# Gathered rows and finished messages in separate buffers in the edge loops of a four-layer graph network, on one core

## The reference, cut to what matters

```python
# layer 0 (the edge's message is a function of both ends and of one edge feature)
x_ = jnp.concatenate([h[src], h[dst], e], axis=1)
m = jax.nn.relu(x_ @ W1 + b1) @ W2 + b2
h_new = jax.ops.segment_sum(m, dst, num_segments=n)

# layer 1
msg = jax.nn.relu(x[src] + edge_attr @ We + be)
aggr = jax.ops.segment_sum(msg, dst, num_segments=n)
h = (1.0 + eps_gin) * x + aggr          # then a small MLP and norms

# layers 2 and 3: x = A x, three and ten times, with A the weighted adjacency
msgs = norm[:, None] * x[row]
x = jax.ops.segment_sum(msgs, col, num_segments=n)
```

## Time and profile before

| | us |
|---|---|
| median of 3 runs | 3231.95 (3231.12 to 3231.97) |
| the profiled execution, its own time | 3232.12 |
| its span in the profile | 3230.3 |
| edge loop of layer 0, 101 superblocks | from about 50 to 1137 |
| edge loop of layer 1, 101 superblocks | from about 1175 to 2194 |
| layers 2 and 3, dense | from about 2260 on |

### The profile page before, as it was taken

How to read it: one execution, slowest core, us unless ns; L and a number is a source line. 1 busy time by engine, 2 the same in 40 slices (tenths; PEclk the granted TensorE clock), 3 DMA queues, 4 the chain that set the end, 5 groups by cost and what they waited for, 6 DMA issues and landing times.

```text
span 3230.3 us, 59857 instructions
## 1 busy us (share of the span) xinstructions
PE 2794.5 (87%) x18663; PEld 1855.0 (57%) x18663; DVE 1793.9 (56%) x3704; ACT 415.6 (13%) x1074; POOL 1158.0 (36%) x1229
## 2 busy tenths in 40 slices
PE   6888888898888858888888888885899999999998
PEld 5677667777777746666666666664333333333333
DVE  4666666666666647777767777774865211111113
ACT  2111111111111111111111111111001000000000
POOL 4355555555555525555555555550000000000000
PEclk9899999989998979999999999996899999999999
DMA  4122222222212232222222222220899999999998
GB/s 115 24 47 48 46 48 48 46 49 46 48 35 46 49 52 60 60 60 60 60 60 60 60 61 61 61 59 5 298 365 337 340 348 343 351 352 353 350 351 279
DMA packets 376595, 447.32 MB, mean 138 GB/s; under 512 B 154575, under 2 KB 193589, under 8 KB 373290
## 3 DMA queue, kind: packets, MB, share of 16 engines
q1 hardware_dynamic: 323834, 376.76, 36.0%
q0 software_dynamic: 38784, 39.79, 6.4%
q10 hardware_dynamic: 13920, 30.00, 2.5%
HBM read 416.03 MB, written 30.36 MB: 138 GB/s over the span
## 4 chain that ended last, share of the span: by engine, by line
PE 44%; issue 18%; SPq 17%; DVE 9%; another core or an unknown queue 8%; DVEq 2%; DMA 1%; ACT 1%; ACTq 0%
PE bank L1652 25%; PE bank L1472 8%; SPq L518 5%; SPq L521 4%; SPq L509 3%; PE bank L1495 3%; SPq L505 2%; PE bank L1625 2%; PE bank L1484 1%; PE bank L1463 1%; DVE arena L860 1%; PE bank L1656 1%; DVE arena L810 1%; SPq L499 1%
## 5 line engine op out<-in xcount | busy, mean ns | idle before, releaser
L1472 PE MATMUL bank<-arena 128*128 128x320 bf16 x6090 | 891.7, 303 | 54.2 <-DVE arena L810 40.4
L1652 PE MATMUL bank<-arena 128*64 128x512 f32 (+1 forms) x4368 | 891.5, 543 | 35.8 <-DVE arena L1062 33.3
L1472 PEld LDWEIGHTS bank<-arena 128*128 128x128 bf16 x6090 | 596.9, 99 | 317.5 <-DVE arena L810 53.6
L646 POOL DMA_INDIRECT arena<-d_p,arena x606 | 572.8, 945 | 539.3 <-issue 384.4
L646 POOL DMA_INDIRECT arena<-d_t,arena x606 | 571.7, 943 | 488.0 <-issue 430.4
L1652 PEld LDWEIGHTS bank<-arena 128*64 128x64 f32 x4368 | 316.2, 136 | 523.0 <-issue 466.1
L817 DVE SCALAR_TENSOR_TENSOR bank<-arena,bank 128x320 f32<-128x320 f32 x404 | 205.8, 553 | 565.6 <-remote 406.6
L1484 PE MATMUL bank<-arena 128*65 128x47 f32 x3232 | 269.6, 234 | 210.1 <-issue 205.2
L1495 PE MATMUL bank<-arena 128*128 128x150 f32 x2352 | 400.6, 328 | 0.0
L1495 PEld LDWEIGHTS bank<-arena 128*128 128x128 f32 x2352 | 387.4, 224 | 7.6 <-issue 0.2
L1484 PEld LDWEIGHTS bank<-arena 128*65 128x65 f32 x3232 | 243.3, 140 | 252.4 <-issue 242.2
(11 more groups left out here) (200 smaller groups left out, 1660.2 us busy)
## 6 DMA issues: line engine op xcount, KB each, us to landing
arena<-d_w SPq DMA_DIRECT2D x312, 1024.0 KB, 8.5
arena<-d_code SPq DMA_DIRECT2D x203, 128.0 KB
d_w<-arena ACTq DMA_DIRECT2D x24, 1024.0 KB
arena<-in_edge_attr SPq DMA_DIRECT2D x101, 128.0 KB
arena<-d_p,arena POOLq DMA_INDIRECT x606
arena<-d_t,arena POOLq DMA_INDIRECT x606
arena<-d_rec SPq DMA_DIRECT2D x588, 4.0 KB
arena<-d_q SPq DMA_DIRECT2D x202, 11.8 KB
```

The source lines that it names most:

```text
L646: g.indirect_dma_start(G[:, b, j, 0:F], None, table, bass.IndirectOffsetOnAxis(ap=idx[:, b, j:j + 1], axis=0)).then_inc(r.g[b], 16)
L1472: last = t.matmul(psY[g], SOH[:, g, a_, :], X[:, a_, z, :, :], start=a_ == z == 0, stop=a_ == SLICES - 1 and z == PARTS - 1)
L1652: last = t.matmul(banks[t_ % 4][F * (n % 2):F * (n % 2) + F, 0:w_], old[:, n, :], right, start=n < 2, stop=False)
```

## The change

The added rows go to a buffer of their own, `M`, and `G` holds only what was gathered:

- `G` gets a pitch of 64 words (two buffers of 8 tiles), and a new `M` of two buffers with pitch `FM` = 65; column 64 of `M` holds what column 64 of `G` held. The space comes from `w1ab`, which moves onto `G`'s place, and from a smaller block of constants.
- DVE's add reads psPre and `G[:, b]` and writes `M[:, b, :, 0:F]`. It waits in addition for `seg[b]` of i-2, because that seg reads `M`.
- POOL's burst of i waits for `add[b]` of i-2 and no longer for its `seg[b]`.
- DVE's select, which writes into `G` too, waits in addition for `add[b]` of i-2 (its own engine).
- ACT's indices of i+2 move ahead of the relu of i, and wait for the landing of the gathers of i (`g[b]`), whose list they overwrite.
- ACT's relu and PE's seg work on `M`.
- At the end of layer 1's loop POOL waits for the gathers and for `agg` before it clears `accL`.

```diff
-        G = at(o_g, 2, 8, FG)
+        G = at(o_g, 2, 8, F)
+        M = at(o_m, 2, 8, FM)
+        w1ab = at(o_g, P)
...
# POOL, superblock
                 pool.wait_ge(r.idx[b], h + 1)
-                pool.wait_ge(r.seg[b], h + 1)
+                pool.wait_ge(r.add[b], h + 1)
...
+            def ordered1():
+                edge_loop(pool, 1, superblock)
+                for b in range(2):
+                    pool.wait_ge(R[1].g[b], 16 * TILES[b][0] * (NSB // 2 + 1 - b))
+                    pool.wait_ge(R[1].agg[b], NSB // 2 + 1 - b + 1)
...
# DVE, select
+                v.wait_ge(r.add[b], h + 1)
...
# DVE, superblock
                 v.wait_ge(r.g[b], 16 * TILES[b][0] * (h + 1))
-                rows_ = G[:, b, :, 0:F]
-                d.tensor_tensor(rows_, psPre.rearrange("p (k f) -> p k f", f=F), rows_, ALU.add).then_inc(r.add[b], 1)
+                v.wait_ge(r.seg[b], h + 1)
+                d.tensor_tensor(M[:, b, :, 0:F], psPre.rearrange("p (k f) -> p k f", f=F), G[:, b], ALU.add).then_inc(r.add[b], 1)
...
# ACT, superblock
+                if exists(r, i + 2):
+                    act.wait_ge(r.g[b], 16 * TILES[b][0] * (h + 1))
+                    indices(r, i + 2, b)
                 act.wait_ge(r.add[b], h + 1 + 1)
-                rows_ = G[:, b, :, 0:F]
+                rows_ = M[:, b, :, 0:F]
                 a.activation(rows_, rows_, ACT.Relu).then_inc(r.relu[b], 1)
-                if exists(r, i + 2):
-                    indices(r, i + 2, b)
...
# PE, superblock
-                    last = t.matmul(psSeg[0:F + 1, 64 * b:64 * b + SPAN], G[:, b, j, 0:F + 1], OH[:, b, j, 0:SPAN],
+                    last = t.matmul(psSeg[0:F + 1, 64 * b:64 * b + SPAN], M[:, b, j, :], OH[:, b, j, 0:SPAN],
```

More of the change, by code:

```diff
@@ L49 @@
 SPAN = 47
-FG = 80
+FM = F + 1
 PIECE = 4
@@ L126, in build @@
         o_ident = take(P)
-        o_w1ab = take(P)
         o_w2 = take(HALF)
@@ L130, in build @@
         o_hi1 = take(PT * NB)
-        o_small = take(111)
+        o_small = take(32)
         o_lo = top[0]
@@ L136, in build @@
         ident = at(o_ident, P)
-        w1ab = at(o_w1ab, P)
         w2p = at(o_w2, HALF)
@@ L142, in build @@
         first = at(o_small + 1, 6, parts=WQ)
-        wcols0 = at(o_small + 25, PW * WIN)
-        first2 = at(o_small + 105, 2)
-        flag = at(o_small + 107, 1, parts=1).bitcast(i32)
-        worst = at(o_small + 108, 1, parts=1)
+        wcols0 = at(o_small + 7, PW * WIN)
+        first2 = at(o_small + 25, 2)
+        flag = at(o_small + 27, 1, parts=1).bitcast(i32)
+        worst = at(o_small + 28, 1, parts=1)
         onesM = ones.to_broadcast([P, P])
@@ L155, in build @@
         o_tab = take(3760)
-        o_g = take(2 * 8 * FG)
+        o_g = take(2 * 8 * F)
+        o_m = take(2 * 8 * FM)
         o_oh = take(2 * 8 * (SPAN + 1))
@@ L674, in _ @@
             pool.wait_ge(s.st_t1, 16)
-            by_order(pool, lambda: general(R[1]), lambda: edge_loop(pool, 1, superblock))
+            def ordered1():
[3 more added lines that the diff above has]
+                    pool.wait_ge(R[1].agg[b], NSB // 2 + 1 - b + 1)
+            by_order(pool, lambda: general(R[1]), ordered1)
             g.memset(accL, 0.0).then_inc(s.consts, 1)
@@ L802, in one_hots @@
                                 iotaP[:, 0:SPAN].unsqueeze(1).to_broadcast([P, 8, SPAN]), ALU.is_equal).then_inc(r.oh[b], 1)
-                beside = OH[:, b][:, :, SPAN:SPAN + 1] if r is R[0] else G[:, b, :, F:F + 1]
+                beside = OH[:, b][:, :, SPAN:SPAN + 1] if r is R[0] else M[:, b, :, F:F + 1]
                 d.tensor_copy(beside, ewflat[:, ds(8 * i, 8)].unsqueeze(2)).then_inc(r.oh[b], 1)
@@ L878, in ordered0 @@
                 for b in range(2):
-                    prep(d.memset(G[:, b, :, F:F + 1], 1.0))
+                    prep(d.memset(M[:, b, :, F:F + 1], 1.0))
                 prep(d.tensor_copy(qtab, qtab0))
```

## The result

| | kernel before | changed kernel |
|---|---|---|
| median | 3231.96 us (4 runs, 3231.12 to 3233.32) | 3826.68 us (4 runs, 3803.37 to 3830.70) |
| profiled execution: own time / span | 3232.12 / 3230.3 us | 3830.70 / 3828.8 us |
| layer 0, first add to last add | 1083.0 us | 1390.1 us |
| layer 1, first add to last add | 997.1 us | 1287.9 us |

The ratio is 1.1825, with a 95% interval of 1.1777 to 1.1873: the change makes the kernel 18% slower. The two loops hold all of it: 307.1 + 290.8 = 597.9 us, of 598.6 us between the two profiled executions.

A forecast was written before the change was run, and what follows sets the result against it. It took a cycle of waits around POOL's gather burst to bound both edge loops. Term 1 (+27 us) and term 2 (+55 us) gave +82 us on 3232.1, forecast as 3312 us, range 3090 to 3480.

The forecast's parts named there:

- What bounds the kernel: Both edge loops: a cycle of waits, release, rest of seg, POOL's start and burst; 9.96 us against 10.02 measured in layer 1.
- What was costed at nothing: The add's new operand place, seg's pitch, DVE's added waits, POOL's wait ending layer 1 and w1ab's new address: 0 us.
- Term 1: On ACT, indices of i+2 wait behind the eviction of i-1: 10.24 us against 9.96, +27 us in layer 1.
- Term 2: In both loops, seg's count falls inside POOL's burst and is held in one superblock of eight: 24 times 2.3, +55 us.
- Most seg counts are held: Rival: both loops lock at 12.7 us or alternate with 10.2; +250 us and more, from 3480 on; chance 0.12.
- Counts pass in the new place: Rival: in both loops PE's counts get through and the kernel is faster, -97 us, 3135 us; chance 0.37.
- SP's slow steps: SP's DMA queue steps take 0.71 us inside any burst, 0.04 outside; cuts the full gain of 213 us to 97.

The follow-up runs named there:

- e1: The changed kernel with POOL's old wait for seg of i-2 put back beside the new one: 3240.3 us, ratio 1.0040 to the kernel before.
- e3: The changed kernel with DVE's source one-hots of i+2 moved ahead of the aggregate's add of i: 3327.24 us.
- e9: The changed kernel run again as it is, in another job: 3737.45 us, ratio 1.1694 to the kernel before.
- e11: The changed kernel with POOL waiting besides for VectorE's second selection product of the next superblock: 3236.16 us; the kernel before took 3195.96.
- e16: The changed kernel with POOL waiting besides for TensorE's count of the previous superblock's gather matmuls: 2732.65 us, ratio 0.9970 to the kernel before.
- e4: The changed kernel with 3 of the 6 gathers of each superblock left out, so it computes something else: 2907.76 us.
- e2: The changed kernel with ACT's indices of i+2 put back behind the relu: 3750.48 us in one execution.

## Why the prediction was wrong

*What bounds the kernel.* Right, for this kind of chip: release, segments, POOL, burst. e1 puts the wait back and gets the old time back.

*What was costed at nothing.* Nearly right: everything but POOL's wait costs 0.4% together (e1), about 13 us, the order on ACT included.

*Term 1, ACT's order, +27 us in layer 1.* The loop exists and has the length that was worked out, 10.36 us against 10.24 (e3). It did not bind, since term 2's loop is longer. In layer 0 it adds a link. In the superblock at 704 ACT's copy of the transposes (L1259) is held until 700.76, so TensorE's product, its pair product (to 705.94), the eviction (706.07) and the indices (706.82) follow late, and the burst starts 3.8 us after the add. In layer 1 all but two bursts start 1.4 us after the add; in layer 0 59 do, and some 40 start up to 4 us later than that. This is where layer 0's 13.81 against layer 1's 12.97 us seems to come from; no run took it apart.

*Term 2, the segment count.* This is the step that failed. The price of a held superblock was right: 12.7 us, and it is 12.97 in layer 1. The number of them was wrong: "one in eight of 194", because a held superblock would push the next gather matmuls ahead and so free itself. Measured, 196 of the 202 segment counts are seen over 1 us late. The traces show no such push. The gather matmuls start behind the one-hots, the one-hots behind the aggregate's add, and the next add, which starts the burst, comes 2.7 to 3.2 us behind the aggregate's add (layer 1) as well: all hang on the same late count, and the next burst starts with them. The place of the count was too early besides. It was put 3.1 us into the burst, with gather matmuls of 4.32 us. With these it is 2.3 to 2.8 in layer 1; but 80 of 98 superblocks have slower ones, and there it is 3.8 to 5.6. No place before 2.3 us occurs in layer 1, so all are late. The lock is not beyond breaking: the changed kernel in e9 has 14 intervals in a row in layer 0 with a mean of 10.5 us, and there the segment count comes 0.9 to 1.7 us into its burst.

Nor was the onset as open as the 1.7 to 4.4 us between two rows made it. The same trace of before, counted over both loops by where in a burst TensorE gave a count, has 17 of 28 late by more than 0.3 us from 2.0 to 2.5 us, 3 of 8 from 3.0 to 3.5, 25 of 26 from 3.5 to 4.0 and 119 of 122 from 4.0 to 4.5 (those from 2.0 to 2.5 are all of the pair product; those from 4.0 on nearly all of gather matmuls). With all held, the prediction's own prices are 27 + 97 x 2.5 = 270 us in layer 1, where 291 were measured, and 97 x 2.1 = 204 us in layer 0, where it was 307: there a held superblock takes 13.81 us and not 12.7. So 474 of the 598 us were within its sums, and it took 82.

*The rivals.* What happened is "Most seg counts are held", with 0.12: from 3480 on, both loops locked near 12.7 us. It named the deciding point that held good (counts are late from less than 3.1 us into a burst on, in the changed kernel 22 of 22 segment counts from 2.5 to 3.0). "Counts pass in the new place" had 0.37, and is what the other kind of chip does: there the changed kernel is 0.3% faster, and the kernel before does not wait either, so most of the gain that this rival forecast was never to be had from the change. SP's slow steps, which it held against the full gain, also belong to the first kind: between 60 and 800 us, 317 of 2481 steps of SP's queue (from one instruction's start to the next) take 0.65 to 0.78 us in the kernel before. On the second kind it is 29 of 3288, in the changed kernel.

*The range.* 3090 to 3480 left the locked loop out on the ground of 0.12. A loop that locks has to be in the range if its deciding point lies within what the rows leave open.

## What to carry to other kernels

Before an engine is let go earlier, write down which counts of other engines will then be given while its work is under way, and when: here the wait that was removed had kept the segment count out of every burst (0 of 202 inside one before, 197 of 202 after), and a wait that put it back in another place (e11) gained 500 us. In a loop whose waits hang on one another a late signal need not be a matter of one time in eight; it can be late each time. See whether the loop brings it into a burst each time, price it at none and at all, and count the late signals of the whole trace by their place before trusting two rows. And time a change that moves signals against DMA bursts on more than one chip, with the kernel before beside it each time.

## What the runs showed that was not expected

- The measurements are of two kinds: the kernel before took 3196 to 3232 us in three measurements and 2739 to 2741 us in three others. On the second kind counts of TensorE inside bursts are seen at once. What makes the difference was not found. The records number the chips, and the same number (5) stood in e1's job (3228 us) and in e16's (2741 us), so it doesn't tell the kind, and I can't say whether it belongs to the chip or to something around it.
- Where counts are late, it starts about 2 us into a burst of gathers and ends with it: 1.6 us after the last of six writes, 1.0 us after the last of three. The gathers' own last packet ends 1.1 us after the last write in the changed kernel and 1.2 us in e4, both in the median, so the end of lateness lies within some 0.5 us of the end of the transfer. TensorE's counts are late to the end of the burst; of VectorE's in e11, all 40 at L840 that are given 2.0 to 2.5 us into one are late, by 0.9 us in the median, while 50 of 50 of its add (L868, 3.0 to 3.5 us into one) and 80 of 80 of L854 (4.0 to 4.5) are seen at once. Why some pair products pass 3 to 4 us into a burst while gather matmuls do not is open.
- Long waits and a low granted clock stand together and last: from 1800 to 2100 us e2 has, but for one, intervals of 13.6 to 14.2 us at a granted clock of 0.85, with 30 gather matmuls in 5.77 us in the superblock shown; from 1490 to 1540 it has shorter ones, 7 to 11 us, with 4.32 us, at 0.94 from 1490 to 1550. In the changed kernel the clock costs nothing of itself: superblocks with gather matmuls at either speed take the same 13 us, since the segment count waits for the end of the burst in both.
